# Where GpSimd sends the third group's rows of the second expert layer: end of the attention block or shared stage

## The reference, cut to what matters

```
logits = xf @ gate_w + gate_b
top_w, top_i = jax.lax.top_k(logits, K)                     # K = 2 of E = 8
gw = jax.nn.softmax(top_w, axis=-1)
combine = (gw[:, :, None] * jax.nn.one_hot(top_i, E)).sum(axis=1)
for e in range(E):
    h = jax.nn.gelu(xf @ w1[e] + b1[e], approximate=False)
    out = out + combine[:, e:e + 1] * (h @ w2[e] + b2[e])
shared = jax.nn.gelu(xf @ ws1 + bs1, approximate=False) @ ws2 + bs2
...
x = x + s4(layernorm(x)); x = x + ffn(layernorm(x))
x = x + attention(layernorm(x)); x = x + ffn(layernorm(x))
```

## Time and profile before

| what | us |
|---|---|
| median of 3 runs (lowest, highest) | 1012.94 (1008.65, 1015.3) |
| span of the profiled execution, first to last instruction | 899.3 |
| front stage, up to the barrier at its end | 0 to 249 |
| attention stage | 250 to 684 |
| shared stage | 685 to 751 |
| last stage | 751 to 899 |

### The profile page before, as it was taken

One profiled execution on the slowest core, in us unless ns is written; L12 is line 12 of the kernel. 1 busy time (PEld: TensorE's weight loads), 2 busy tenths in 40 slices (PEclk: granted clock), 3 DMA queues, 4 the chain that ended last, 5 costly groups with the idle time before them and its releaser, 6 DMA issues. The chain is left out here.

```text
span 899.3 us, 21979 instructions
## 1 busy us (share of the span) xinstructions
PE 633.2 (70%) x7826; PEld 468.5 (52%) x7826; DVE 635.0 (71%) x1395; ACT 445.1 (49%) x873; POOL 456.7 (51%) x569
## 2 busy tenths in 40 slices
PE   0197973882059999324799998998963795999950
PEld 0073432562049999312566665665641564998850
DVE  6989988681048888387677777877741972888855
ACT  5632167670035555271766665665642242555534
POOL 1126767887637777510002222554573881677760
PEclk9978997896579999755899999999985997999985
DMA  9510001432134563242121322332111412454418
GB/s 287 132 37 1 0 0 45 83 80 58 44 60 90 102 93 84 85 162 60 45 83 50 91 73 73 78 105 74 49 36 37 80 34 48 84 97 93 93 27 281
DMA packets 131850, 70.51 MB, mean 78 GB/s; under 512 B 89535, under 2 KB 118725, under 8 KB 131746
## 3 DMA queue, kind: packets, MB, share of 16 engines
q1 hardware_dynamic: 121042, 50.46, 23.8%
q0 software_dynamic: 9088, 16.88, 6.9%
q10 hardware_dynamic: 1616, 1.77, 0.7%
HBM read 26.61 MB, written 30.50 MB: 64 GB/s over the span
## 5 line engine op out<-in xcount | busy, mean ns | idle before, releaser
L1437 ACT ACTIVATE ARENA<-banks,ARENA 128x256 f32<-128x256 f32 x312 | 122.2, 474 | 104.2 <-PE banks L1400 86.7
L2150 DVE TENSOR_REDUCE ARENA<-banks 128x4 f32<-128x1024 f32 (+1 forms) x128 | 122.7, 959 | 46.7 <-PE banks L1891 45.4
L1398 PE MATMUL banks<-ARENA,W1H 128*128 128x256 f16 x312 | 87.1, 279 | 65.3 <-DMA ARENA<-slots 58.2
L2072 ACT ACTIVATE ARENA<-banks 128x1536 f32<-128x1536 f32 x64 | 92.8, 1450 | 58.2 <-PE banks L1919 58.2
L1412 PE MATMUL banks<-W2L,ARENA 128*128 x624 | 110.8, 220 | 3.2 <-DVE ARENA L1450 2.4
L1414 PE MATMUL banks<-W2H,ARENA 128*128 x624 | 110.2, 219 | 0.0
L1413 PE MATMUL banks<-W2H,ARENA 128*128 x624 | 110.1, 219 | 0.0
L1388 POOL DMA_INDIRECT expert_out_g<-ARENA x78 | 80.6, 1034 | 47.7 <-issue 25.8
L1388 POOL DMA_INDIRECT expert_out_f<-ARENA x78 | 80.0, 1026 | 37.5 <-issue 25.8
L1471 DVE TENSOR_TENSOR ARENA<-ARENA 128x1024 f16<-128x1024 f32 x78 | 95.6, 1226 | 2.7
L1000 POOL DMA_INDIRECT slots<-ARENA,PLACE x64 | 77.6, 1212 | 28.4 <-issue 20.4
(11 more groups left out here) (312 smaller groups left out, 1812.0 us busy)
## 6 DMA issues: line engine op xcount, KB each, us to landing
spread<-ARENA SPq DMA_DIRECT2D x96, 64.0 KB, 2.1
ARENA<-expert_out_f SPq DMA_DIRECT2D x8, 512.0 KB, 7.4
ARENA<-spread SPq DMA_DIRECT2D x16, 256.0 KB, 3.0
ARENA<-spread SPq DMA_DIRECT2D x32, 128.0 KB, 3.0
ARENA<-expert_out_g SPq DMA_DIRECT2D x8, 512.0 KB, 7.3
XT<-in_w SPq DMA_DIRECT2D x10, 256.0 KB, 7.7
slots<-EMPTY SPq DMA_DIRECT2D x16, 129.0 KB, 4.5
ARENA<-in_w SPq DMA_DIRECT2D x8, 256.0 KB, 6.8
```

What stands on the lines that cost most here:

```text
L1398: pe.matmul(out, t.W1H[:, e, ms], XST[i][:, 0], start=True, stop=False)
L1437: ins = nc.scalar.activation(HF[i % 2][:, m], UP[i % 2][:, m], ACT.Gelu, bias=BIAS[i % 4][:, m:m + 1], scale=1.0 / WS)
L2072: nc.scalar.activation(PR[x % 2], t.psum_all[:, 5:8, :], ACT.Exp, scale=1.0 / LOGIT).then_inc(exps, 1)
L2150: dve.tensor_reduce(MX[:, G // 2, tile, :, :, G % 2].rearrange("p s a -> p a s"), src, AX.X, ALU.max).then_inc(m_red, 1)
```

## The change

The third group (group 2, tiles 16 to 23) is sent in the attention stage instead of in the shared stage: `SENT_IN_ATTENTION` goes from 2 to 3. By the old rule the group's first piece would fall to `c` = 14, the last of the loop, and its other three pieces to batches that the loop doesn't reach. So at `c` = 14 the loop sends nothing, and all four pieces are sent behind it, after the rows of batch 14 and ahead of the wait for what was sent:

```
-SENT_IN_ATTENTION = ROUTED_IN_ATTENTION - 1
+SENT_IN_ATTENTION = ROUTED_IN_ATTENTION
...
-                for g in range(SENT_IN_ATTENTION):
+                for g in range(SENT_IN_ATTENTION if c < NB - 2 else 0):
                     piece = c - 4 * g - 6
...
             batches.rows(pool, NB - 2)
+            for g in range(SENT_IN_ATTENTION):
+                late = range(NB - 2 - 4 * g - 6, 4)
+                for piece in late:
+                    if piece in (0, 1):
+                        route.dispatch_first(pool, g, range(GRP // 2 * piece, GRP // 2 * piece + GRP // 2))
+                    if piece in (2, 3):
+                        route.dispatch_second(pool, g, (piece - 2,))
             route.sent_all(pool, SENT_IN_ATTENTION)
```

## The result

| | kernel before | kernel after |
|---|---|---|
| median of 4 runs, us | 1010.8 (1007.03 to 1015.3) | 1025.41 (1018.95 to 1032.69) |
| ratio, 95% interval | | 1.0142 (1.0075 to 1.021) |

What follows compares the result with a forecast made beforehand. GpSimd was taken to end both the attention and the shared stage; +23.3 us in the first and -5.2 us in the second gave +18.1 us, moving the median from 1012.94 to 1031 us, range 1024 to 1037.

Steps and rivals of the forecast that it cites:

- Who ends each stage: GpSimd ends the attention stage, 3.9 us behind the next engine, and the shared stage by only 5.2 us.
- Start and 16 DMAs: Attention stage's end: 0.42 us extra at the start, then 20.2 us for 16 DMAs and two iotas on GpSimd.
- Landing: Attention stage's end: GpSimd waits 1.57 us after the last DMA's issue before its drain starts.
- The drain, the fourth step: Attention stage's end: 82 to 84 ns per indirect DMA since the last drain, so 10.4 us for 126 DMAs.
- The shared stage: Group 3 starts earlier, VectorE becomes last with 4.5 us of cover over GpSimd: -5.2 us.
- The sum: Whole span: 23.3 us lost in attention less 5.2 us gained in the shared stage, +18.1 us.
- The first, that the drain is old work and the dispatch hides it: Rival at the attention stage's end: only 1.3 us of drain remains, sum +9.1 us, 1022 us; chance 8%.
- The second, VectorE freed: Rival in the shared stage: VectorE's chain shortens by about 8 us or more, at most 15.4 us; chance 2%.
- The third, no gain in the shared stage: Rival: GpSimd stays last in the shared stage, the whole +23.3 us loss remains, 1036 us; chance 6%.

Runs made afterwards that it cites:

- the second trace of before: The kernel before, unchanged, run and traced again beside the kernel after: 1002.1 us in its one run.
- the early drain: A GpSimd drain added behind the attention stage's 78 sends of results: in the kernel after ratio 1.0133, in the kernel before 0.9994, repeated 0.9992.
- the second measurement: Kernel before and kernel after, both unchanged, timed again on one chip: 1015.12 us after against 1002.9 before, ratio 1.0101.
- the DMAs put back: The kernel after, but the shared stage sends group 2 once more: 1017.1 us against 1002.9 for the kernel before, ratio 1.0142.
- one piece moved: The kernel before with a GpSimd drain behind the 78 sends and only group 2's first four DMAs at the attention block's end: ratio 1.0006, repeated 0.9975.
- the kernel with 114: The kernel after with only group 2's first 4 DMAs in the attention stage and all 16 in the shared stage: single time 1017.22 us.

## Why the prediction was right or wrong

**Who ends each stage: right.** GpSimd at the attention block's end and, by a few microseconds only, at the shared block's end; the second trace of before says the same (3.9 and 4.2 us).

**Start and 16 DMAs: right.** 0.42 + 20.2 = 20.62 us were taken from the front stage's quiet group, 20.68 were measured. Choosing the quiet row over the 31.0 us of the shared stage, because VectorE was out by then, was what this term hung on. SyncE was not done, as the prediction had it of the other engines: it drained 6.2 us behind the rows work (748.8), and the DMAs beside it took no longer.

**Landing: right.** 1.57 us forecast, 764.8 - 763.25 = 1.55 measured.

**The drain, the fourth step: wrong in size.** 10.4 us forecast for 126 DMAs, 4.47 measured. The step carried "82 to 84 ns for each indirect DMA since the last one" from four stages with 32 to 110 DMAs to one with 126. The price for each further DMA holds on both sides, and that the count starts at the last drain is shown by the early drain (78 in the middle, 48 or 32 at the end). What fails is the straight line through the origin: from 114 DMAs on the drain is as short as if 72 fewer were counted, and why is open. The attention stage so lost 17.4 us in place of 23.3. These 5.9 us are most of the 6.6 us by which the sum is off; the other 0.7 are the shared stage's.

**The shared stage: right in who ends it, the size in part by luck.** -5.2 us forecast with VectorE as the next bound, -5.9 measured. GpSimd's group 3 took 30.5 us (31.0 taken), its drain 1.37 us (1.3), and it was out 4.1 us ahead of VectorE (4.5). But in the second trace of before GpSimd was only 4.2 us behind VectorE (5.2 in the earlier trace rows); the other 1.7 of the 5.9 us are VectorE's own end, 61.8 us behind the attention block's end before and 60.1 after. In the third trace with 16 DMAs, that with the early drain, it came at 62.6. All nine traces with 32 DMAs there have a shared stage of 65.8 to 67.2 us, the three with 16 have 60.1, 60.3 and 62.6. What moves VectorE's end is not shown.

**The sum.** +18.1 forecast; +11.5 by the terms of two traces, +14.6 between the medians of the first measurement, +12.2 in the second (10.1 by its ratio). The sign was settled by the 22 us of dispatch, which no engine covers: even a drain of nothing would have left the attention stage 13 us longer (22.2 less 9.2), more than the shared stage gives back. The 1031 us stand on 1012.94 and on the drain that was too long. That 1025.41 is inside the range is in part luck: on 1012.94 the terms as measured give 1024.4, and the ratio of the second measurement 1023.2.

**The rivals.** The first, that the drain is old work and the dispatch hides it, would have left 1.3 us and a sum of +9.1, which the times alone could not tell from what was measured. The drain's row does: 4.47 us. The drain did come out shorter than before, which that rival alone foretold in kind. But with waiting as the cause the drain should shorten as the dispatch grows, and it is the reverse: 4 DMAs in 6.91 us leave 3.49 us, 16 in 22.2 us leave 4.47. It fell by one step, between 112 and 114 DMAs; whether their number or SyncE's end sets it is open. The second, VectorE freed, falls too, as VectorE's end came 0.9 us earlier between the first traces, 1.7 between the second, and not 8: line 1259 of the kernel after reads

```profile
L1259 DVE TENSOR_TENSOR ARENA<-ARENA x8: 2291/2293/2293, 780.5 to 823.6; 128x2048 f16<-128x2048 f32 x8
```

which is the earlier trace rows again with 16 DMAs fewer beside it. The third, no gain in the shared stage, falls by the order of the drains there; only with the DMAs put back did it come about.

**The page on the drain.** The Trainium skill (VectorE: DVE Perf Modes, section "The DRAIN you can't avoid") has drains of about 12 ns on all five engines, and it places them in a kernel's preamble and postamble. Where the kernel after starts, the trace agrees for four engines with 7 to 10 ns, while GpSimd's drain there took 187 ns. The drains at the blocks' ends stand elsewhere, so the prediction carried the figure to a place that the page does not speak of; GpSimd's took 9.04 us before and 4.47 after.

**Left open.** What makes the drain fall between 112 and 114 DMAs, their number or SyncE's end ahead of it, and in what time the 72 are done; no run here shows work or waiting for it. And whether the gains of 4 us seen in traces, with the early drain or one piece moved, exist in time. The same drain in the middle with other counts than 78 wasn't tried.

## What to carry to other kernels

An engine that is free on average is not free at a barrier: before work is moved ahead of one, look at which engine's drain comes last there and what lies between it and the next; everything put behind the last engine's work is paid in full, while what leaves the other stage is paid back only as far as the second engine allows (22 us against 6 here). If GpSimd must be relieved by a few microseconds at a stage's end, move the few DMAs that the next engine's margin is worth, not a whole group, and look for a long wait into which its drain can be put; both shortened the traces here, and neither is shown to shorten the time. A cost that is a straight line through four sizes is an estimate beyond the largest of them: take a fall off the line into the range too.

## What the runs showed of the hardware

GpSimd's drain takes 82 to 85 ns for each indirect DMA that it has sent since its last drain, from 16 (1.37 us) over 28, 32, 36, 48, 64 and 78 to 112 (9.20 us). In the kernel with 114 it is 3.49 us, and it grows again at 82 ns for each, to 4.47 us at 126, as if 72 were taken off; that the number does this is not shown. A drain of 6.4 us put into a wait for VectorE left that wait as long as it was (10.52 against 10.48 us) and the next drain then counts only the DMAs behind it (32 and 2.67 us in the kernel before, 48 and 3.98 in the kernel after).
